# Moving the next batch's projections and its q transfer ahead inside an attention and FFN kernel

## The chip, the cores and the metric

One core of a Trainium2 chip runs the kernel. The metric is the device time of one execution in microseconds.

## The reference

Four batches of 512 tokens with 128 channels pass through one transformer block: layer norm, attention with 16 heads of 8 channels, a residual, layer norm, a mixture FFN whose eight experts are all computed, and a residual.

```python
qkv = (x @ w_attn + b_attn).reshape(b, t, 3, H, D).transpose(2, 0, 3, 1, 4)
scores = jnp.einsum('bhtd,bhsd->bhts', q, k) / jnp.sqrt(jnp.float32(D))
scores = scores + slopes[None, :, None, None] * pos[None, None, None, :]
attn = jax.nn.softmax(jnp.where(causal[None, None], scores, -jnp.inf), axis=-1)
y = jnp.einsum('bhts,bhsd->bhtd', attn, v)            # then @ w_proj + b_proj
x = x + attention(layernorm(x))
logits = xf @ gate_w.T + gate_b                       # xf = layernorm(x), rows of 128
logits = logits * rsqrt(mean(logits * logits) + eps) * rms_w
g = top_1(softmax(logits / 0.5)); norm_g = g / (g + 1e-6)
h = gelu(einsum('nd,edh->neh', xf, w1) + b1); y = einsum('neh,ehd->ned', h, w2) + b2
x = x + (y * norm_g[:, None, None]).sum(axis=1)
```

## The kernel before

The work is laid out by hand. A batch has four steps (s = 0 to 3), one for each set of four heads, and each step has 16 places. Tables say at which place each engine takes which piece: the two plans give the twelve units of maxima, the twelve units of scores and exponentials and the three kinds of attention times v; `STAGES` (L72) gives the stages that come once per batch as (step, place, batches behind; -1 is the next batch). Every engine walks the same tables in its own program, so an engine's order is fixed and all coupling is through semaphores.

In a step, TensorE computes raw scores of the next step's heads for the row maxima (`max_unit`, L720, into three banks `v_ring` which VectorE empties at L1047), transposes the maxima (L729), and computes this step's scores again (`exp_unit`, L742 and L748, into three banks `a_ring`) for ScalarE's exponentials (L553), then multiplies them with v (L767). The negated maxima take part in the scores as rows of `q_stack`: VectorE writes `m_hi` and `m_lo` (L1064, L1065), SP sends them with `load_max` (L385), and the first scores of the next step, at its place 4, wait for them. FFN tiles of an earlier batch (L673 to L675 into `a_ring`, gelu at L570, L835) are spread over the steps from batch 1 step 1 on: five in a step, but one in each step 2.

The next batch's x is prepared on the way. VectorE takes its statistics (`x_stats`, L958), GpSimd the inverse root (`x_rstd`, fourteen small operations at L330 to L341), VectorE normalises (`x_norm`, L967), TensorE transposes (`x`, L684) and projects (`k` and `q` at L673 to L675, `v` the same lines in twelve small products), VectorE evacuates (L950, L951, L1019, L1011, L1033). q and k are split into a high part (ScalarE, L594, at the units of `SCALAR_STAGES`) and a low part (GpSimd, `split_low`, L442). They go to the operands `q_stack` (two buffers) and `k_stack` (one) by DMA: `load_q` (L366, 256 KB each: the high part twice and the low part once; from batch 2 on also 64 KB of zeros, L362, ahead), `load_k` on SP for the high key parts (L324, eight of 32 KB for each half of the heads) and `load_k_low` on GpSimd (L324, four of 32 KB). The first half of `k_stack` is free for the next batch when all scores of steps 0 and 1 are out. The first maxima of the next batch stand at place 0 of step 3 and wait for q and both key parts.

SP's program inside the loop is `load_k(b, 1)`, `load_residual(b)`, `load_x(b + 1)` in step 0; `store(b - 2)` in step 1, which waits for the result of the stage `ffn` at place 14 of that step; the loads of the next batch in step 2; and `load_max` at the end of each step. GpSimd's has `load_k_low(b, 1)` and the inverse root of z in step 0 and, in step 1, `x_rstd`, both `split_low` and `norm_logits(b - 1)` (L330 to L341, L482, L483), which waits for the logits of place 4 of step 2; then `load_k_low(b + 1, 0)` and `residual(b)` in step 2.

Of the kernel before, what the change touches and what calls it, by code (L numbers as in the profile page):

```python
# [71 lines left out]
STAGES = {  # L72
    "y_low": (2, 14, 0), "y_high": (0, 4, 1), "y_norm": (0, 5, 1), "attention": (0, 7, 1),
    "z_norm": (0, 13, 1), "z": (0, 15, 1), "logits": (2, 4, 1), "route": (2, 13, 1), "gates": (3, 13, 1),
    "ffn": (1, 14, 2), "x_stats": (0, 15, -1), "x_norm": (1, 7, -1), "x": (1, 10, -1), "k": (1, 12, -1),
    "q": (1, 15, -1), "v": (1, 14, -1), "b2": (2, 15, 0),
}

SCALAR_STAGES = {
    "k_high": (1, 7, -1), "q_high": (1, 11, -1), "gates": (3, 1, 1),  # L80
}


# [14 lines left out]
def block_kernel(nc, x, w_attn, w_proj, w1, w2, columns, rows, consts, out):  # L98
    B, T, C = x.shape
# [19 lines left out]
    with ExitStack() as ctx:  # L119
# [169 lines left out]
        def next_set(b, s):  # L289

            return (b, s + 1) if s < SETS - 1 else (b + 1, 0)
# [29 lines left out]
        def send_k(queue, part, half, g, q, loaded):  # L321

            rows = QR * q + half * QR // 2
            queue.dma_start(k_stack[QR * g + q * D:QR * g + (q + 1) * D, 2 * half:2 * half + 2, q, :].bitcast(F32),  # L324
                            part[rows:rows + QR // 2, :].bitcast(F32)).then_inc(loaded, 16)

        def inverse_sqrt(engine, settle, y, src, scale, eps, v, t, fused=False):


            settle(engine.tensor_scalar(v, src, scale, eps, ALU.mult, ALU.add))  # L330
            settle(engine.tensor_scalar(y.bitcast(I32), v.bitcast(I32), -0.5, float(RSQRT_GUESS), ALU.mult, ALU.add))
            for _ in range(3):
                if fused:
                    settle(engine.scalar_tensor_tensor(out=t, in0=y, scalar=-0.5, in1=y, op0=ALU.mult, op1=ALU.mult))
                    settle(engine.tensor_tensor(t, t, v, ALU.mult))
                    settle(engine.scalar_tensor_tensor(out=y, in0=t, scalar=1.5, in1=y, op0=ALU.add, op1=ALU.mult))
                else:
                    settle(engine.tensor_tensor(t, y, y, ALU.mult))
                    settle(engine.tensor_tensor(t, t, v, ALU.mult))
                    settle(engine.tensor_scalar(t, t, -0.5, 1.5, ALU.mult, ALU.add))  # L340
                    settle(engine.tensor_tensor(y, y, t, ALU.mult))  # L341
# [4 lines left out]
        @block.sync  # L346
        def _(sp):
            def load_x(b):
                if b >= 1:
                    sp.wait_ge(xn_ready, b)  # L350
                sp.dma_start(x_in[:], x_view[b]).then_inc(x_loaded, 16)

            def load_residual(b):
                if b >= 1:
                    sp.wait_ge(xb_ready, b)
                sp.dma_start(x_res[:], x_view[b]).then_inc(xres_loaded, 16)

            def load_q(b):

                if b >= 2:  # L360
                    sp.wait_ge(e_filled, UNITS * SETS * (b - 1))
                    sp.dma_start(q_stack[b % 2][MAX_ROWS:MAX_ROWS + 2 * QUADS, :, :].bitcast(F32),  # L362
                                 zeros[0:2 * QUADS * SETS, :]).then_inc(q_loaded, 16)
                for g, part in ((0, 0), (1, 0), (2, 1)):
                    sp.wait_ge(q_split, 2 * b + part + 1)
                    sp.dma_start(q_stack[b % 2][QR * g:QR * (g + 1), :, :].bitcast(F32),  # L366
                                 (q_hi, q_lo)[part][:].bitcast(F32)).then_inc(q_loaded, 16)

            def load_k(b, half):


                if b == 0:
                    sp.wait_ge(k_zeros, half + 1)
                else:

                    sp.wait_ge(e_filled, UNITS * (SETS * (b - 1) + 2 * half + 2))
                sp.wait_ge(k_split, 2 * b + 1)
                for q in range(QUADS):
                    for g in (0, 2):
                        send_k(sp, k_hi, half, g, q, k_loaded[half][q])  # L380

            def load_max(b, s):
                sp.wait_ge(m_ready, SETS * b + s + 1)
                for r, part in ((MAX_ROWS, m_hi), (MAX_ROWS + QUADS, m_lo)):
                    sp.dma_start(q_stack[b % 2][r:r + QUADS, s, :].bitcast(F32),  # L385
                                 part[:].bitcast(F32)).then_inc(m_loaded, 16)

            def store(b):
                sp.wait_ge(result_ready, b + 1)
                sp.dma_start(out_view[b], result[:]).then_inc(stored, 16)  # L390

            load_x(0)
            sp.dma_start(w_attn_sb[:], w_attn).then_inc(wa_loaded, 16)
            sp.dma_start(cst[:], consts).then_inc(cst_loaded, 16)
            sp.dma_start(cols_sb[:], columns).then_inc(rows_loaded, 16)
            sp.dma_start(rows_sb[:], rows.to_broadcast([P, rows.shape[1]])).then_inc(rows_loaded, 16)
            sp.dma_start(w1_sb[:], w1).then_inc(w1_loaded, 16)
            load_q(0)
            load_k(0, 0)
            load_k(0, 1)  # L400
            sp.dma_start(w_proj_sb[:], w_proj).then_inc(wp_loaded, 16)
            sp.dma_start(w2_sb[:], w2).then_inc(w2_loaded, 16)
            load_residual(0)
            load_x(1)
            load_max(0, 0)
            for b in range(B):
                for s in range(SETS):
                    if s == 0 and b >= 1:
                        load_k(b, 1)
                        load_residual(b)  # L410
                        if b + 1 < B:
                            load_x(b + 1)
                    if s == 1 and b >= 2:
                        store(b - 2)
                    if s == 2 and b + 1 < B:
                        load_k(b + 1, 0)
                        load_q(b + 1)
                    if next_set(b, s)[0] < B:
                        load_max(*next_set(b, s))
            store(B - 2)  # L420
            store(B - 1)
            sp.wait_ge(stored, 16 * B)
# [3 lines left out]
        def _(pool):  # L426
# [22 lines left out]
            def load_k_low(b, half):  # L449

                if b == 0:
                    pool.wait_ge(k_zeros, half + 1)
                else:

                    pool.wait_ge(e_filled, UNITS * (SETS * (b - 1) + 2 * half + 2))
                pool.wait_ge(k_split, 2 * b + 2)
                for q in range(QUADS):
                    send_k(pool, k_lo, half, 1, q, k_low_loaded[half][q])
# [3 lines left out]
            def settle(ins):  # L462

                steps[0] += 1
                ins.then_inc(pool_step, 1)
                pool.wait_ge(pool_step, steps[0])
# [11 lines left out]
            def norm_logits(b):  # L478

                pool.wait_ge(square_ready, b + 1)  # L480
                inverse_sqrt(pool, settle, inverse_rms[:], mean_square[:], 1.0 / E, EPS_F32, var[:, 0, :], var[:, 1, :])
                settle(pool.tensor_tensor(lg2[:], lg[:], inverse_rms[:].unsqueeze(2).to_broadcast([P, TB, E]), ALU.mult))  # L482
                pool.tensor_tensor(lg[:], lg2[:], rms_rows.unsqueeze(1).to_broadcast([P, TB, E]),  # L483
                                   ALU.mult).then_inc(logits_normed, 1)
# [29 lines left out]
            for b in range(B):  # L514
                for s in range(SETS):
                    if s == 0 and b >= 1:
                        load_k_low(b, 1)
                        z_rstd(b - 1)
                    if s == 1 and b + 1 < B:
                        x_rstd(b + 1)  # L520
                        split_low(b + 1, 0)
                        split_low(b + 1, 1)
                    if s == 1 and b >= 1:
                        norm_logits(b - 1)
                    if s == 2 and b + 1 < B:
                        load_k_low(b + 1, 0)
                    if b == 0 and s == 0:
                        pool.wait_ge(w1_loaded, 16)
                        split(w1_sb[:], w1_hi[:], w1_lo[:], w1_split, 0)
                        pool.wait_ge(rows_loaded, 32)  # L530
                        split(gate_sb, gate_parts[:, 0:E], gate_parts[:, E:2 * E], w1_split, 2)
                    if s == 2:
                        residual(b)
# [744 lines left out]
```

## Time and profile before

| what | value |
|---|---|
| median of 3 runs | 341.61 us (341.31 to 342.7) |
| profiled execution, span | 341.4 us |
| TensorE busy | 295.9 us (87%) |
| VectorE busy | 192.6 us (56%) |
| ScalarE busy | 193.7 us (57%) |
| GpSimd busy | 84.1 us (25%) |
| mean granted clock of TensorE | 0.949 |
| idle of TensorE ahead of L720, until the low key parts landed | 15.3 us in 3 stretches, the longest 8.9 |

The span runs from the first to the last instruction of one execution. Busy shares are of the whole span. An idle time is put down to what came last. The longest of the three stretches is in the start of the kernel. The engines are named PE (TensorE), PEld (its weight loads), DVE (VectorE), ACT (ScalarE), POOL (GpSimd) and SP (SyncE); a q behind the name is the engine's sequencer.

### The profile page before, as it was taken

How to read it: one execution, taken by the hardware profiler on the slowest of the kernel's cores; microseconds unless marked ns; L12 is line 12 of the kernel's file. 1: busy time of each engine (PE TensorE's matmuls, PEld its weight loads, DVE VectorE, ACT ScalarE, POOL GpSimd, SP SyncE). 2: the span in 40 equal slices, each digit the busy share in tenths (PEclk: the TensorE clock that was granted, in tenths of full speed). 3: DMA queues.
4: the chain of work that ended last, by engine and by line, in shares of the span. 5: the costliest groups of instructions: out<-in, count | busy, mean ns of one | idle time of the engine just before them, and what ended most of it. 6: DMA issues, size and time to landing. Idle time of an engine off the chain costs nothing.

```text
span 341.4 us, 5507 instructions
## 1 busy us (share of the span) xinstructions
PE 295.9 (87%) x1784; PEld 193.8 (57%) x1784; DVE 192.6 (56%) x787; ACT 193.7 (57%) x322; POOL 84.1 (25%) x213
## 2 busy tenths in 40 slices
PE   0245899997979999699999997899999999998994
PEld 0133466565556676466766765557756665655661
DVE  5624759776786867145677776264867741161111
ACT  1871064463455568275759467376667788634462
POOL 8569203240233027002033126002210220000030
PEclk9985579999999999699999999899999999999999
DMA  7166500070120006200300028001100100000101
GB/s 198 66 90 96 193 2 2 16 122 9 38 74 4 0 19 105 29 2 18 95 1 4 0 61 120 3 2 44 35 4 2 35 2 2 0 2 0 31 1 31
DMA packets 12380, 13.29 MB, mean 39 GB/s; under 512 B 2048, under 2 KB 9088, under 8 KB 12096
## 3 DMA queue, kind: packets, MB, share of 16 engines
q1 hardware_dynamic: 11328, 11.90, 16.1%
q0 software_dynamic: 1024, 1.05, 1.9%
q8 instruction: 14, 0.23, 0.3%
q14 instruction: 14, 0.11, 0.1%
HBM read 5.21 MB, written 1.05 MB: 18 GB/s over the span
## 4 chain that ended last, share of the span: by engine, by line
PE 74%; DVE 12%; DMA 7%; issue 3%; ACT 1%; POOL 1%; DVEq 0%; SPq 0%; ACTq 0%; POOLq 0%
PE ffn_bank L835 16%; PE a_ring L742 11%; PE v_ring L720 11%; PE pv_bank L767 9%; DMA k_stack<-k_lo 6%; PE a_ring L673 5%; DVE unused L1047 5%; PE a_ring L748 5%; PE a_ring L674 4%; PE a_ring L675 4%; DVE xn L967 2%; PE v_ring L796 1%; PE v_ring L729 1%; DMA x_in<-x 1%; PE v_ring L673 1%
## 5 line engine op out<-in xcount | busy, mean ns | idle before, releaser
L1047 DVE CUSTOM_DVE_ANT_0 unused<-v_ring,cst 128x512 bf16<-128x512 f32 (+3 forms) x256 | 112.1, 487 | 68.5 <-PE v_ring L720 63.9
L553 ACT ACTIVATE probs<-a_ring 128x512 f32<-128x512 f32 (+1 forms) x192 | 92.5, 526 | 74.7 <-PE a_ring L748 73.5
L720 PE MATMUL v_ring<-k_stack,q_stack 128*128 128x512 f32 (+3 forms) x256 | 89.6, 422 | 20.2 <-DMA k_stack<-k_lo 15.3
L742 PE MATMUL a_ring<-q_stack,k_stack 128*128 128x512 f32 (+3 forms) x256 | 76.8, 360 | 0.4 <-DMA q_stack<-m_lo 0.4
L720 PEld LDWEIGHTS v_ring<-k_stack,q_stack 128*128 128x128 f32 x256 | 49.5, 210 | 40.6 <-issue 23.5
L570 ACT ACTIVATE hidden<-a_ring,cols_sb 128x512 f32<-128x512 f32 x64 | 43.4, 688 | 43.2 <-PE a_ring L675 42.7
L835 PE MATMUL ffn_bank<-hidden,w_sb 128*128 128x512 f32 x128 | 66.3, 602 | 1.1 <-ACT ffn_T L579 0.8
L742 PEld LDWEIGHTS a_ring<-q_stack,k_stack 128*128 128x128 f32 x256 | 46.7, 197 | 7.8 <-issue 4.0
L748 PE MATMUL a_ring<-score_mask,ident_bf 128*128 128x128 bf16 (+1 forms) x192 | 48.1, 252 | 0.0
L767 PE MATMUL pv_bank<-probs,v_ones 128*32 128x256 f32 (+3 forms) x512 | 43.2, 447 | 0.0
L673 PE MATMUL a_ring<-zT_hi,w_hi 128*128 128x512 f32 x64 | 34.2, 534 | 0.8 <-DVEq L953 0.8
L324 POOL DMA_DIRECT2D k_stack<-k_lo x32 | 18.1, 568 | 61.3 <-PE a_ring L748 60.5
L748 PEld LDWEIGHTS a_ring<-score_mask,ident_bf 128*128 128x128 bf16 x192 | 18.7, 98 | 20.6 <-issue 14.0
L674 PE MATMUL a_ring<-zT_lo,w_hi 128*128 128x512 f32 x64 | 26.1, 407 | 0.0
L675 PE MATMUL a_ring<-zT_hi,w_lo 128*128 128x512 f32 x64 | 25.9, 405 | 0.0
L835 PEld LDWEIGHTS ffn_bank<-hidden,w_sb 128*128 128x128 f32 x128 | 21.5, 192 | 5.9 <-ACT hidden L570 3.1
L1047 DVE DVE_READ_ACCUMULATOR2_ANT row_max<- 128x1 f32 x256 | 21.3, 83 | 0.0
L673 PEld LDWEIGHTS a_ring<-zT_hi,w_hi 128*128 128x128 f32 x64 | 12.7, 199 | 12.3 <-issue 7.9
L330 POOL TENSOR_SCALAR var<-mean_square 128x4 f32<-128x4 f32 x4 | 0.8, 193 | 73.8 <-DVE mean_square L1113 73.8
L767 PEld LDWEIGHTS pv_bank<-probs,v_ones 128*32 128x32 f32 x512 | 12.4, 110 | 10.0 <-issue 7.0
L570 ACT ACT_TABLE_LOAD x13 | 16.7, 1283 | 0.2
L674 PEld LDWEIGHTS a_ring<-zT_lo,w_hi 128*128 128x128 f32 x64 | 12.8, 200 | 5.0 <-issue 3.6
(109 smaller groups left out, 298.4 us busy)
## 6 DMA issues: line engine op xcount, KB each, us to landing
q_stack<-q_hi SPq DMA_DIRECT2D x8, 256.0 KB
k_stack<-k_hi SPq DMA_DIRECT2D x64, 32.0 KB
x_in<-x SPq DMA_DIRECT2D x4, 256.0 KB, 3.6
hidden<-w SPq DMA_DIRECT2D x1, 1024.0 KB, 8.3
q_stack<-q_lo SPq DMA_DIRECT2D x4, 256.0 KB
k_stack<-k_lo POOLq DMA_DIRECT2D x32, 32.0 KB, 4.0
w_sb<-w SPq DMA_DIRECT2D x1, 1024.0 KB, 5.2
x_res<-x SPq DMA_DIRECT2D x4, 256.0 KB, 3.1
```

The lines of the kernel that those rows point to most:

```text
L324: queue.dma_start(k_stack[QR * g + q * D:QR * g + (q + 1) * D, 2 * half:2 * half + 2, q, :].bitcast(F32), part[rows:rows + QR // 2, :].bit ...
L553: act.activation(probs[:, n % 2, q, KIND_AT[kind]:KIND_AT[kind] + cols], a_bank()[:, 0:cols], ACT.Exp).then_inc(e_freed, 1)
L570: act.activation(hidden[:, n % HB, :], a_bank()[:], ACT.Gelu, bias=b1_cols[:, m:m + 1]).then_inc(g_freed, 1)
L673: pe.matmul(dst, lhs[0], rhs[0], start=True, stop=False)
L674: pe.matmul(dst, lhs[0], rhs[1], start=False, stop=False)
L675: return pe.matmul(dst, lhs[1], rhs[0], start=False, stop=True)
L720: last = pe.matmul(dst[:, at:at + P * (n + 1)], q_stack[b % 2][:, s, n * P:(n + 1) * P], k_stack[:, s, q, 0:P * (n + 1)], start=True, stop ...
L742: pe.matmul(dst[:, at:at + P * (TB - j)], k_stack[:, s, q, j * P:(j + 1) * P], q_stack[b % 2][:, s, j * P:T], start=(at == 0), stop=False, ...
L748: pe.matmul(diagonal, ident_bf[:], score_mask[:].unsqueeze(1).to_broadcast([P, blocks, P]), start=False, stop=True, skip_group_check=True) ...
L767: last = pe.matmul(pv_bank[QR * q:QR * (q + 1), j * P:T], v_ones[b % 2][:, j, s, q, :], probs[:, n % 2, q, at:at + cols], start=(s % 2 == ...
L835: pe.matmul(ffn_bank[:], w2_sb[:, m, :], hidden[:, n % HB, :], start=(m == 0), stop=(m == NT - 1)).then_inc(ffn2_done, 1)
L1047: ins = dve.tensor_tensor_reduce(unused[:, (uses[0] - 1) % V_BANKS, at:at + cols], bank_[:, at:at + cols], cst[:, C_MASK + T - cols:C_MASK ...
```

## The change

The next batch's stages move: the statistics from place 15 of step 0 to place 9, the normalisation from place 7 of step 1 to place 0, the transpose from 10 to 3, k from 12 to 5, q from 15 to 7, v from 14 to 10; the high parts on ScalarE move from behind unit 7 (k) and 11 (q) of step 1 to behind units 2 and 4. SP sends q in step 1, behind the store and ahead of the maxima, where it sent it in step 2 behind the high key parts. GpSimd sends the low key parts ahead of the normalisation of the logits.

```diff
-    "ffn": (1, 14, 2), "x_stats": (0, 15, -1), "x_norm": (1, 7, -1), "x": (1, 10, -1), "k": (1, 12, -1),
-    "q": (1, 15, -1), "v": (1, 14, -1), "b2": (2, 15, 0),
+    "ffn": (1, 14, 2), "x_stats": (0, 9, -1), "x_norm": (1, 0, -1), "x": (1, 3, -1), "k": (1, 5, -1),
+    "q": (1, 7, -1), "v": (1, 10, -1), "b2": (2, 15, 0),
 }
 
 SCALAR_STAGES = {
-    "k_high": (1, 7, -1), "q_high": (1, 11, -1), "gates": (3, 1, 1),
+    "k_high": (1, 2, -1), "q_high": (1, 4, -1), "gates": (3, 1, 1),
 }
...
                     if s == 1 and b >= 2:
                         store(b - 2)
+                    if s == 1 and b + 1 < B:
+                        load_q(b + 1)
                     if s == 2 and b + 1 < B:
                         load_k(b + 1, 0)
-                        load_q(b + 1)
                     if next_set(b, s)[0] < B:
                         load_max(*next_set(b, s))
...
-                    if s == 1 and b >= 1:
-                        norm_logits(b - 1)
                     if s == 2 and b + 1 < B:
                         load_k_low(b + 1, 0)
+                    if s == 2 and b >= 1:
+                        norm_logits(b - 1)
```

## Rows read from the trace of the kernel before

**Rows 1.** The page: its first line, and the granted clock in 40 slices.

```profile
span 341.4 us, 5507 instructions
...
PEclk9985579999999999699999999899999999999999
```

**Rows 2.** Timeline, TensorE: start us, us, what, idle before and releaser.

```profile
79.00 0.70 PE L720 MATMUL v_ring<-k_stack,q_stack 128*128 128x512 f32 x3 [2.77 <-issue]
...
139.70 1.19 PE L720 MATMUL v_ring<-k_stack,q_stack 128*128 128x512 f32 x3 [3.12 <-DMA k_stack<-k_lo]
...
214.57 1.19 PE L720 MATMUL v_ring<-k_stack,q_stack 128*128 128x512 f32 x3 [3.22 <-DMA k_stack<-k_lo]
```

**Rows 3.** Timeline, GpSimd: the issue of batch 2's low key parts.

```profile
133.49 2.27 POOL L324 DMA_DIRECT2D k_stack<-k_lo  x4 [0.32 <-PE a_ring L748]
```

**Rows 4.** Windows: busy us of PE, PEld, DVE, ACT, POOL; granted clock; DMA; GB/s.

```profile
139.00:140.00 1.00, 0.30 (x1) 0.33 (x2) 0.00 (x0) 0.00 (x0) 0.00 (x0) 0.64 0.02 4
...
146.00:147.00 1.00, 1.00 (x6) 0.85 (x5) 0.02 (x1) 0.82 (x2) 0.00 (x0) 0.95 0.00 0
...
217.00:218.00 1.00, 1.00 (x4) 0.76 (x4) 0.00 (x0) 0.00 (x0) 0.00 (x0) 0.61 0.00 0
```

**Rows 5.** Timeline, the SP queue: issues.

```profile
72.17 0.61 SPq L366 DMA_DIRECT2D q_stack<-q_lo  x1
...
196.63 0.39 SPq L390 DMA_DIRECT2D out<-result  x1
...
204.67 0.67 SPq L362 DMA_DIRECT2D q_stack<-zeros  x1
...
206.67 0.60 SPq L366 DMA_DIRECT2D q_stack<-q_lo  x1
```

**Rows 6.** Timeline, TensorE and VectorE, batch 2, steps 1 and 2.

```profile
194.79 0.30 PE L673 MATMUL v_ring<-w_attn_hi,xT_hi 128*128 128x128 f32 x1
...
195.33 1.13 DVE L1136 SCALAR_TENSOR_TENSOR result<-v_ring,gate,x 128x128 f32<-128x128 f32 x4 [0.26 <-DVE m_lo L1065]
...
196.16 1.07 PE L835 MATMUL ffn_bank<-hidden,w_sb 128*128 128x512 f32 x2
...
197.24 0.48 PE L673 MATMUL v_ring<-xT_hi,w_attn_hi 128*128 128x512 f32 x1
...
198.03 0.63 PE L720 MATMUL v_ring<-k_stack,q_stack 128*128 128x512 f32 x3
...
203.40 0.44 PE L742 MATMUL a_ring<-q_stack,k_stack 128*128 128x512 f32 x1
```

**Rows 7.** Chain near 39 us; DMA issues with us to landing, 30:45, then 90:100.

```profile
39.26 1.91 DMA q_stack<-m_lo
...
x_in<-x SPq DMA_DIRECT2D x1, 256.0 KB, 5.6
...
x_in<-x SPq DMA_DIRECT2D x1, 256.0 KB, 3.1
```

**Rows 8.** Timeline, VectorE, batch 1, end of step 0.

```profile
98.57 0.69 DVE L1047 CUSTOM_DVE_ANT_0 unused<-v_ring,cst 128x512 bf16<-128x512 f32 x1
...
101.80 1.12 DVE L967 TENSOR_SCALAR z<-x,mv,rstd 128x128 f32<-128x128 f32 x4 [0.33 <-POOLq L476]
...
105.40 0.87 DVE L958 BATCH_NORM_STATS2 stats<-x_in 128x6 f32<-128x128 f32 x4 [0.32 <-DVE zT_lo L951]
...
106.61 0.66 DVE L1047 CUSTOM_DVE_ANT_0 unused<-v_ring,cst 128x512 bf16<-128x512 f32 x1
```

**Rows 9.** Timeline, batch 0, end of step 1 and step 2.

```profile
63.29 0.28 DVE L1065 SCALAR_TENSOR_TENSOR m_lo<-v_ring,m_hi 16x128 fp32r<-16x128 f32 x1
...
65.09 0.75 DVE L1011 TENSOR_SCALAR q_full<-v_ring,cols_sb 128x512 f32<-128x512 f32 x1 [0.32 <-PE v_ring L675]
...
67.11 1.28 POOL L442 TENSOR_TENSOR q_lo<-q_full,q_hi 128x512 fp32r<-128x512 f32 x1 [2.26 <-ACT q_hi L594]
...
68.29 0.44 PE L742 MATMUL a_ring<-q_stack,k_stack 128*128 128x512 f32 x1
```

## The prediction

> **What bounds the kernel now.** I read the page first, then the idle time of TensorE in the timeline around each start of a batch's work, then the SP and GpSimd queues there, then the clock by windows. The span is 341.4 us and the granted clock is low only at the start and in two short dips [rows 1]; TensorE is busy 87% of the span, so what matters is where it stands still. It does so at one place of each batch: step 3, place 0, where the first maxima of the next batch need that batch's q and k in SBUF. The idle times in brackets are 2.77, 3.12 and 3.22 us for next batches 1, 2 and 3, so it stopped at 76.23, 136.58 and 211.35 [rows 2]. The releaser named is the low key parts: GpSimd issues them only at 133.49, as it first normalised the logits of the batch before [rows 3]. But SP sends q late too: from the issue of its low part to TensorE's restart it is 6.83 us at batch 1 (72.17 to 79.00) and 7.90 us at batch 3 (206.67 to 214.57) [rows 2, 5]. Both have to come earlier, and the change moves both.
>
> In the two later stalls the clock fell to 1.2 GHz (0.5 of full). Window 139 to 140 has a mean of 0.64, which puts the fall at 139.3, 2.7 us after the stop; the windows at 146 and 217 put the return at 146.1 and 217.8 [rows 4]. From restart to return that is 6.4 and 3.2 us at half speed, in which TensorE is the bound: 3.2 and 1.6 us lost.
>
> **What the change gives.** q, k and v leave places 12 to 15 of step 1 for 5, 7 and 10, q is issued in step 1, and the low key parts no longer wait for the logits. The key parts then go out when the last scores of step 1 are done, some 12 us ahead of the stop. SP's eight issues of high key parts follow the maxima's, as before. None of these is last at step 3 any more. Stalls: 2.77 + 3.12 + 3.22 = 9.1 us. Clock: 3.2 + 1.6 = 4.8 us. Span 341.4 - 13.9 = 327.5 us if nothing takes their place. Behind the stalls the next limit is TensorE itself: ScalarE and VectorE were idle in them. The number of instructions is the same on every engine. GpSimd's normalisation of the logits now follows four key issues, and its reader stands at place 13 of step 2, so it costs nothing.
>
> **What it costs, part by part.** I take the edits in order of time.
>
> *Batch 0, step 1.* This step has no FFN tiles and VectorE nearly fills it. v and q ran behind the maxima (the negated maxima end at 63.57; v at 63.89, q at 65.09, 0.88 and 0.75 us with gaps of 0.3 us) and now run ahead of them, 2.2 us; the statistics of 1.2 us leave the step and add some 0.5 us to the one before. So the negated maxima are ready at about 65.1. q's part on VectorE ends five maxima units and v ahead of them, some 5 us, at 60.2; from its end to the end of GpSimd's low part was 2.55 us (65.84 to 68.39), so SP issues that part at about 62.8 and it is usable 6.83 us later, at 69.6. The maxima, issued at 65.3, lie behind it in SP's queue. The first scores of step 2 need them and started at 68.29 [rows 5, 9]. Cost 1.3 us; bounds 0 (the end of VectorE's excess is covered) and 2.5.
>
> *Batch 1, step 0.* The statistics of the next x move from place 15 to place 9. On VectorE they take from 105.40 to the next operation at 106.61, 1.2 us. Place 9 comes there at 98.57. What follows is tight: the maxima, then z at 101.80 after only 0.33 us of idle, and TensorE waited for z [rows 8]. So z comes some 1.3 us later, and with it TensorE's next FFN tiles. Bounds 0.9 (the 0.33 us absorb a part) and 2.1 (x not yet landed when its statistics come; x takes 3.1 us there [rows 7]).
>
> *Batch 2, step 0, and the order inside the steps 1 with FFN tiles.* There VectorE has gaps and TensorE is the bound. ScalarE takes the high key parts after unit 2 and may wait a little for VectorE, with three banks of scores as a cover. I put 0.4 us, bounds -0.5 and 1.5.
>
> *Batch 2, step 1: the store.* This is the large one. In SP's program the store of batch 0's result stands ahead of the new q loads, and it waits for the FFN result of place 14. Before, only the maxima of step 2 stood behind it. Now the store, the zeros, q's three transfers and then the maxima leave in this order, though q itself has long been ready. The result op ran at 195.33 and the store went at 196.63. v and q now stand ahead of it on TensorE, which has no idle time there: v takes 194.79 to 196.16, 1.37 us, and q 197.24 to 198.03, 0.79 us [rows 5, 6]. So the store goes at 198.8, the zeros at 199.2, and the low q part 2.0 us later (204.67 to 206.67 before [rows 5]), at 201.2. By the two distances of the first paragraph q is usable at 208.1 to 209.1. The maxima were issued behind it. If they land behind it, the first scores of step 2, which started at 203.40 [rows 6], wait until 208.7: 5.3 us, bounds 4.7 and 5.8. If they pass it, they go at 201.9 and 202.6 and land 1.91 us later [rows 7], at 204.5: 1.1 us. For the first speaks that a 256 KB load of x takes 5.6 us on this queue behind a 1 MB load and 3.1 us without [rows 7]; I take 5.3. TensorE has nothing else to do in that time, and 5.3 us is longer than the 2.7 us after which the clock fell before, so I add the mean of the two losses, 2.4 us (bounds 1.6 and 3.2). Sum 7.7 us; this batch alone loses what its old stall cost (3.2 + 1.6) and more.
>
> The Trainium skill (DMA: Bandwidth & Descriptors, section Queues, rings and completion order) says that on each DMA engine descriptors are consumed in ring order, and that SP has one ring on each of the engines. By that rule the maxima's packets wait behind q's, and this case's x rows agree (5.6 against 3.1 us); it speaks against putting q ahead of the maxima. By the rule the sum would be the forecast, without it the time of the first rival.
>
> At batch 1 there is no store ahead. There q's part on VectorE also ends five maxima units and v ahead of the maxima, as in batch 0, and the step holds five FFN tiles more, so I put nothing.
>
> **Sum.** 327.5 + 1.3 + 1.3 + 0.4 + 7.7 = 338.2 us of span. The median of the runs, 341.61, is 0.2 above the profiled span, so 338.4 us.
>
> **Rivals.**
> *The maxima pass q* (or the store comes early enough): in batch 2 the cost is 1.1 us without a clock fall: 338.4 - 4.2 - 2.4 = 331.8 us. For it: the maxima are 8 KB and no row shows them behind q with a reader waiting. Against: the x rows. Chance 0.2. It reaches down to 328 if the costs of batches 0 and 1 are nil as well.
> *The clock falls in batch 1 too.* With z 1.3 us later, two idle stretches follow each other around 98 to 104. The clock held through 2.77 us of idle at batch 1's stall, as the page's clock line shows no dip there [rows 1, 2], but these two are close together. Price 1.6 to 3.2: 340.8 us. Chance 0.12.
> *SP is held at q in every batch* (slower). If the low q part is ready not 5 us ahead of the maxima, but 2 us behind them, because ScalarE's high part or GpSimd's low part is late, then SP stands at that wait with the maxima ready behind it. At batch 0 the low part goes at 67.1 and the scores at 73.9: 5.6 instead of 1.3 us. At batch 1, by the distances of batch 2's rows (maxima ready at 195.1 + 2.2, q part at 199.2, usable at 207.1, scores at 203.40), 3.7 us and a clock fall of 2.4. Sum 338.4 + 4.3 + 6.1 = 348.8 us. It decides as soon as the q part is later than the maxima by about 0.5 us. Against it: on VectorE q is five units and v ahead of the maxima. Chance 0.06.
> *The stalls stay,* because something else is last at step 3 (the high key parts, eight issues of SP that follow the maxima). They would have to be some 4 us later than I put them. In batch 2, where SP is late with them, TensorE is late as well. One of the two larger stalls kept, with its clock, gives 338.4 + 3.1 + 3.2 = 344.7 us. Chance 0.04.
>
> **How the numbers follow.** Forecast 338.4 us, chance 0.58, own range 336 to 340.5. The range for 8 in 10 reaches to the first and second rival: 330.5 to 341.5. A measurement of this kernel can tell about 0.5% from no change, so faster is below 339.9 and slower above 343.3. Faster: nearly all of the forecast, the first rival and a third of the second, 0.83. Slower: 0.07. Within: 0.10.
>
> **What would show it.** Right: no idle time of TensorE at step 3, place 0, in any batch; key issues of GpSimd right behind the last scores of step 1; in batch 2 the store some 2 us later than its place now, and then an idle stretch of about 5 us ahead of the first scores of step 2 with the maxima's transfer as releaser, and a clock dip behind it; in batch 1 z 1.3 us later in its step. Wrong: if that stretch is 1 us, packets pass each other in SP's queue; if TensorE still waits at step 3, a key part is last; if the steps 1 of batches 0 and 1 show waits of the scores for maxima longer than 2 us, the third rival holds.

## The result and the profile after

The changed kernel takes 342.52 us (median of 20 runs, 339.45 to 345.44) and the kernel before 341.69 us (20 runs); the ratio, from which executions over 1.5% above the fastest of their kernel are left out, is 1.005 with a 95% interval of 1.0028 to 1.0073, and that of the two medians is 1.002. So it is slower, by half a per cent or less. The forecast was 338.4 us, faster by 1%, with a range up to 341.5. Two parts of the page of the changed kernel, for [rows 1]: the totals, TensorE's busy share in 40 slices and the granted clock in tenths of full speed.

```profile
span 341.0 us, 5507 instructions
...
PE 298.7 (88%) x1784; PEld 195.8 (57%) x1784; DVE 190.3 (56%) x787; ACT 194.9 (57%) x322; POOL 84.7 (25%) x213
...
PE   0607999799959999999999929999999999998994
...
PEclk9965599989998999999999976999999999999999
```

The span is even 0.4 us shorter than in the profile of before, 341.0 against 341.4 us. That is an accident of the start, which the change does not touch: the first scores of batch 0 came at 41.30 us in the profile of before and at 37.9 to 38.6 us in that of every other kernel of this text. So the two profiles have to be compared step by step. The table has the start of the first scores of each step (the first product of `exp_unit`, at place 4), read from the timeline, and the interval since the one ahead. Below, an interval is named by the batch and step at whose first scores it ends: (2, 2) is the 18.59 us up to the first scores of batch 2, step 2.

| batch, step | before, us | interval | after, us | interval | difference |
|---|---|---|---|---|---|
| 0, 0 | 41.30 | | 38.03 | | |
| 0, 1 | 53.78 | 12.48 | 51.09 | 13.06 | +0.6 |
| 0, 2 | 68.29 | 14.51 | 67.45 | 16.36 | +1.9 |
| 0, 3 | 81.29 | 13.00 | 79.26 | 11.81 | -1.2 |
| 1, 0 | 91.57 | 10.28 | 89.54 | 10.28 | 0.0 |
| 1, 1 | 110.45 | 18.88 | 111.53 | 21.99 | +3.1 |
| 1, 2 | 128.63 | 18.18 | 129.44 | 17.91 | -0.3 |
| 1, 3 | 148.80 | 20.17 | 143.56 | 14.12 | -6.1 |
| 2, 0 | 166.12 | 17.32 | 160.88 | 17.32 | 0.0 |
| 2, 1 | 184.81 | 18.69 | 180.01 | 19.13 | +0.4 |
| 2, 2 | 203.40 | 18.59 | 204.60 | 24.59 | +6.0 |
| 2, 3 | 222.19 | 18.79 | 221.79 | 17.19 | -1.6 |
| 3, 0 | 239.51 | 17.32 | 239.11 | 17.32 | 0.0 |

Behind (3, 0) the two agree to 0.1 us a step. The differences add up to +2.9 us. The medians differ by 0.8 us only: the profile of before was a quick execution but for its start, and the part on the sum says what is known of that.

The stalls at step 3 are gone, as meant. The two sums of TensorE's idle time by releaser (us in total, times, longest) show what came for them: of the key parts only the wait in the kernel's start is left, and the scores now wait for the maxima.

```profile
PE v_ring L721 <- DMA k_stack<-k_lo: 8.9, 1, 8.9
...
PE a_ring L743 <- DMA q_stack<-m_lo: 8.5, 3, 6.1
```

This is step 3, place 0 of batch 1, which answers to the second line of [rows 2]: the products of the maxima follow the products with v without idle time.

```profile
136.32 1.07 PE L768 MATMUL pv_bank<-probs,v_ones 128*32 128x384 f32 x16
...
137.32 0.74 PE L721 MATMUL v_ring<-k_stack,q_stack 128*128 128x512 f32 x3
```

And these are the places where TensorE waits instead (timeline; the idle time ahead of each in brackets): the first scores of (0, 2); the transposes of the maxima and of z at the end of batch 1's step 0; the last maxima ahead of, and the first scores of, (2, 2).

```profile
67.45 0.49 PE L743 MATMUL a_ring<-q_stack,k_stack 128*128 128x512 f32 x1 [1.94 <-DMA q_stack<-m_lo]
...
99.70 0.28 PE L730 MATMUL v_ring<-cst,row_max 128*16 128x128 f32 x1 [1.09 <-DVEq L1057]
...
102.10 1.12 PE L805 MATMUL v_ring<-cst,z 128*128 128x128 f32 x4 [1.45 <-DVE z L968]
...
197.68 0.80 PE L721 MATMUL v_ring<-k_stack,q_stack 128*128 128x384 f32 x2
...
204.60 0.80 PE L743 MATMUL a_ring<-q_stack,k_stack 128*128 128x512 f32 x1 [6.12 <-DMA q_stack<-m_lo]
```

In batch 1 only the 1.09 us ahead of the maxima's transpose are new. The wait for z is as long in the profile of before, where it had no fall of the clock:

```profile
102.97 0.66 PE L804 MATMUL v_ring<-cst,z 128*128 128x128 f32 x4 [1.45 <-DVE z L967]
```

The wait ahead of (2, 2) is the store's. VectorE's result op and SP's queue behind it, for [rows 5, 6]:

```profile
192.26 1.13 DVE L1137 SCALAR_TENSOR_TENSOR result<-v_ring,gate,x 128x128 f32<-128x128 f32 x4 [0.27 <-PE v_ring L843]
```

```profile
193.57 0.39 SPq L390 DMA_DIRECT2D out<-result  x1
194.01 0.70 SPq L362 DMA_DIRECT2D q_stack<-zeros  x1
194.75 1.24 SPq L366 DMA_DIRECT2D q_stack<-q_hi  x2
196.04 0.60 SPq L366 DMA_DIRECT2D q_stack<-q_lo  x1
196.69 0.68 SPq L385 DMA_DIRECT2D q_stack<-m_hi  x1
197.41 0.85 SPq L385 DMA_DIRECT2D q_stack<-m_lo  x1
```

The store goes 0.2 us behind the result, then the zeros, q and the maxima, in one row. The maxima, issued at 196.69 and 197.41, are usable at 204.60. In the chain that ended last their second part takes 7.15 us there and 3.77 us in batch 0:

```profile
63.64 3.77 DMA q_stack<-m_lo
...
197.41 7.15 DMA q_stack<-m_lo
```

And the clock falls at each of the three places: in batch 0 0.4 us after TensorE's restart, in the other two while TensorE still waits. The windows, for [rows 4], have the granted clock third from the end:

```profile
core 0: us, PE busy (x) PEld busy (x) DVE busy (x) ACT busy (x) POOL busy (x), PEclk, DMA share, GB/s
...
67.00:68.00 1.00, 0.55 (x3) 0.40 (x3) 0.00 (x0) 0.00 (x0) 0.00 (x0) 0.91 0.17 37
...
71.00:72.00 1.00, 1.00 (x10) 0.92 (x8) 0.71 (x5) 0.49 (x2) 0.00 (x0) 0.89 0.14 33
...
101.00:102.00 1.00, 0.00 (x0) 0.00 (x0) 1.00 (x4) 0.98 (x2) 0.68 (x4) 0.97 0.00 0
...
102.00:103.00 1.00, 0.90 (x5) 0.90 (x5) 0.05 (x1) 0.44 (x1) 0.75 (x4) 0.50 0.06 16
...
105.00:106.00 1.00, 1.00 (x20) 0.38 (x12) 1.00 (x3) 0.00 (x0) 0.00 (x0) 0.82 0.00 0
...
200.00:201.00 1.00, 0.00 (x0) 0.00 (x0) 0.00 (x0) 0.00 (x0) 0.69 (x4) 0.97 1.07 127
...
201.00:202.00 1.00, 0.00 (x0) 0.00 (x0) 0.00 (x0) 0.00 (x0) 0.70 (x4) 0.50 1.05 129
...
211.00:212.00 1.00, 1.00 (x10) 0.92 (x8) 0.76 (x4) 0.71 (x2) 0.00 (x0) 0.91 0.00 0
```

It is at 0.5 from about 67.8 to 71.2, from 101.9 to 105.4, and from 200.9 to 211.2 us.

### The profile page after: what moved, and what is told of

Same layout as the page of the kernel before. It is cut to its first block, busy times and chain, and to the rows that moved or that the text cites. A ratio compares the mean times of both kernels' runs of the same rounds, so it can differ in the third digit from the quotient of the medians.

```text
span 341.0 us, 5507 instructions
## 1 busy us (share of the span) xinstructions
PE 298.7 (88%) x1784; PEld 195.8 (57%) x1784; DVE 190.3 (56%) x787; ACT 194.9 (57%) x322; POOL 84.7 (25%) x213
## 3 DMA queue, kind: packets, MB, share of 16 engines
q1 hardware_dynamic: 11328, 11.90, 16.3%
## 4 chain that ended last, share of the span: by engine, by line
PE 71%; DMA 8%; DVE 8%; SPq 4%; ACT 4%; issue 3%; POOL 2%; DVEq 0%; ACTq 0%; POOLq 0%
PE ffn_bank L836 15%; PE a_ring L743 11%; PE v_ring L721 10%; PE pv_bank L768 9%; PE a_ring L674 5%; PE a_ring L749 4%; PE a_ring L676 4%; PE a_ring L675 4%; DMA q_stack<-m_lo 4%; DVE unused L1048 4%; DMA k_stack<-k_lo 2%; DMA cst<-consts 2%; SPq L324 2%; ACT k_stack L604 1%; PE v_ring L674 1%
## 5 line engine op out<-in xcount | busy, mean ns | idle before, releaser
L554 ACT ACTIVATE probs<-a_ring 128x512 f32<-128x512 f32 (+1 forms) x192 | 93.9, 526 | 90.6 <-PE a_ring L749 89.4
L721 PE MATMUL v_ring<-k_stack,q_stack 128*128 128x512 f32 (+3 forms) x256 | 91.9, 430 | 11.1 <-DMA k_stack<-k_lo 8.9
L743 PE MATMUL a_ring<-q_stack,k_stack 128*128 128x512 f32 (+3 forms) x256 | 78.9, 369 | 8.5 <-DMA q_stack<-m_lo 8.5
L721 PEld LDWEIGHTS v_ring<-k_stack,q_stack 128*128 128x128 f32 x256 | 50.9, 216 | 31.3 <-issue 21.6
L743 PEld LDWEIGHTS a_ring<-q_stack,k_stack 128*128 128x128 f32 x256 | 48.2, 203 | 16.8 <-DMA q_stack<-m_lo 8.5
L749 PE MATMUL a_ring<-score_mask,ident_bf 128*128 128x128 bf16 (+1 forms) x192 | 49.2, 257 | 0.0
L674 PE MATMUL a_ring<-zT_hi,w_hi 128*128 128x512 f32 x64 | 33.0, 516 | 0.8 <-DVEq L954 0.8
L675 PE MATMUL a_ring<-zT_lo,w_hi 128*128 128x512 f32 x64 | 25.1, 393 | 0.0
L675 PEld LDWEIGHTS a_ring<-zT_lo,w_hi 128*128 128x128 f32 x64 | 12.1, 189 | 4.9 <-issue 3.6
```

The lines of the kernel that those rows point to most:

```text
L554: act.activation(probs[:, n % 2, q, KIND_AT[kind]:KIND_AT[kind] + cols], a_bank()[:, 0:cols], ACT.Exp).then_inc(e_freed, 1)
L674: pe.matmul(dst, lhs[0], rhs[0], start=True, stop=False)
L675: pe.matmul(dst, lhs[0], rhs[1], start=False, stop=False)
L721: last = pe.matmul(dst[:, at:at + P * (n + 1)], q_stack[b % 2][:, s, n * P:(n + 1) * P], k_stack[:, s, q, 0:P * (n + 1)], start=True, stop ...
L743: pe.matmul(dst[:, at:at + P * (TB - j)], k_stack[:, s, q, j * P:(j + 1) * P], q_stack[b % 2][:, s, j * P:T], start=(at == 0), stop=False, ...
L749: pe.matmul(diagonal, ident_bf[:], score_mask[:].unsqueeze(1).to_broadcast([P, blocks, P]), start=False, stop=True, skip_group_check=True) ...
```

## The experiments

Each run is told by the intervals of the table above where its profile decides, and by its time beside runs of the kernel before on the same chip.

**1. q ahead of the store.** The changed kernel with two calls exchanged in SP's step 1:

```diff
+                    if s == 1 and b + 1 < B:
+                        load_q(b + 1)
                     if s == 1 and b >= 2:
                         store(b - 2)
-                    if s == 1 and b + 1 < B:
-                        load_q(b + 1)
```

> The changed kernel with one edit: in step 1, SP sends the next batch's q ahead of the store instead of behind it. Theory A (in batch 2 the store holds q, so that the maxima end up behind 832 KB of q traffic): the 6.12 us of idle ahead of the first scores of batch 2's step 2 and the clock dip behind it go; that step's interval falls from 24.6 to about 18.6 us and the next from 17.2 to about 14; time about 342.5 - 9 = 333.5 us. The waits of batch 0 (1.94 us) and of batch 1 stay. Rival B (the maxima are late by themselves, because v and q stand ahead of them on TensorE): the store's place changes nothing, 4 us or more of idle stay and the time is above 338 us.

Measured: 333.12 us against 340.51 of before, ratio 0.976 (0.971 to 0.981). The intervals of (2, 2) and (2, 3) fall from 24.59 and 17.19 to 18.31 and 14.11 us, 9.4 us together, and no idle time is left there. The wait of batch 0 stays, as expected, and the clock dip behind it was longer in this profile ((0, 3) is 13.17 us):

```profile
68.29 0.80 PE L743 MATMUL a_ring<-q_stack,k_stack 128*128 128x512 f32 x1 [2.20 <-DMA q_stack<-m_lo]
```

So the place of the store alone turns the changed kernel from 0.5% slower into 2.4% faster.

**2. q behind the maxima.** The changed kernel with q still in step 1, but behind the maxima:

```diff
-                    if s == 1 and b + 1 < B:
-                        load_q(b + 1)
...
                     if next_set(b, s)[0] < B:
                         load_max(*next_set(b, s))
+                    if s == 1 and b + 1 < B:
+                        load_q(b + 1)
```

> The changed kernel with SP sending the next batch's q in step 1 behind the maxima of that step instead of ahead. Theory A (the maxima wait behind q in SP's queue in batches 0 and 2): both idle times ahead of the first scores of step 2 go (1.94 and 6.12 us) with their clock dips; q still lands before step 3 in batches 1 and 2, and within 1 us of it in batch 0; about 331.5 us. Rival: q and with it the high key parts, now behind it, land too late for step 3, and stalls of 1 to 3 us come back there in each batch with clock dips: 336 to 340 us.

Measured: 329.62 us, ratio 0.966 (0.961 to 0.971). (0, 2) is 14.56 us instead of 16.36, (0, 3) 10.25 instead of 11.81; batch 2 is as in the first run; no stall at step 3. The maxima of batch 0 did wait behind q. What is left is mostly in batch 1, where (1, 1) is 22.24 us against 18.88 before. The page's clock line shows a dip there and nowhere else:

```profile
PEclk9999999999997999999999999999999999999999
```

**3. GpSimd's order alone.** The kernel before, with the low key parts ahead of the normalisation of the logits, everything else as it was:

```diff
-                    if s == 1 and b >= 1:
-                        norm_logits(b - 1)
                     if s == 2 and b + 1 < B:
                         load_k_low(b + 1, 0)
+                    if s == 2 and b >= 1:
+                        norm_logits(b - 1)
```

> The kernel before with the GpSimd part of the change alone: low key parts sent ahead of the normalisation of the logits; stages and SP's order as before. Theory A (two transfers are late at step 3, and q's low part is as late as the low key parts): the stalls stay at 2.8 to 3.2 us, perhaps 1 us shorter as key and q traffic no longer meet; 340 to 341.7 us. Rival (the low key parts alone were last, as the page names them): the stalls of batches 1 and 2 and their clock dips go, 8 us less, about 333.5 us.

Measured: 338.39 us against 340.51, ratio 0.991 (0.988 to 0.995). The three stalls are all there, 0.4 to 0.5 us shorter in batches 1 and 2, and those two are now put down to q's low part:

```profile
75.63 0.70 PE L720 MATMUL v_ring<-k_stack,q_stack 128*128 128x512 f32 x3 [2.77 <-issue]
...
137.56 0.73 PE L720 MATMUL v_ring<-k_stack,q_stack 128*128 128x512 f32 x3 [2.73 <-DMA q_stack<-q_lo]
...
210.60 0.97 PE L720 MATMUL v_ring<-k_stack,q_stack 128*128 128x512 f32 x3 [2.68 <-DMA q_stack<-q_lo]
```

So the releaser that the page named in [rows 2] was only the last of two: the other transfer, q's low part, was 0.4 to 0.5 us earlier. Behind the first stall the clock fell, which it had not done in the profile of before: the page's clock line shows it, and (1, 0) is 11.77 us instead of 10.28.

```profile
PEclk9965599997999999799999999799999999999999
```

**4. Late statistics.** The run with q behind the maxima, and all moved stages some places later:

```diff
-"x_stats": (0, 9, -1), "x_norm": (1, 0, -1), "x": (1, 3, -1), "k": (1, 5, -1), "q": (1, 7, -1), "v": (1, 10, -1)
+"x_stats": (0, 15, -1), "x_norm": (1, 3, -1), "x": (1, 6, -1), "k": (1, 8, -1), "q": (1, 10, -1), "v": (1, 12, -1)
-"k_high": (1, 2, -1), "q_high": (1, 4, -1)
+"k_high": (1, 5, -1), "q_high": (1, 7, -1)
```

> The run with q behind the maxima, and the next batch's stages three places later: statistics back at place 15 of step 0, normalisation 3, transpose 6, k 8, q 10, v 12 of step 1, high parts behind units 5 and 7. Theory A (the statistics at place 9 delay z in batch 1 and with it bring the clock dip there): batch 1's interval from the first scores of step 0 to those of step 1 falls from 22.0 to about 19.2 us, the clock dip near 102 us goes, 2.8 us less than with the stages of the change. Rival (the clock dip there is chance, or comes from the rest of the change): no more than 1.2 us less.

Measured: 337.97 us (eight runs, one of them 422.1 us), ratio 0.989 (0.985 to 0.994), 8 us slower than the run it started from. In batch 1 it did as expected: (1, 1) is 18.87 us, 3.4 less. But (0, 2) is 22.79 us instead of 14.56, and (1, 2) and (2, 2) are 1.9 and 1.7 us longer. In batch 0 the statistics' root isn't ready at place 3, VectorE stands with the maxima behind it, TensorE with it; the clock is at half for about 10 us there (0.50 in all windows from 54 to 62 us). The maxima are late again ahead of the scores:

```profile
54.76 1.09 PE L685 MATMUL v_ring<-cst,xn 128*128 128x128 f32 x4 [2.91 <-DVE row_max L1048]
...
73.27 0.50 PE L743 MATMUL a_ring<-q_stack,k_stack 128*128 128x512 f32 x1 [1.73 <-DMA q_stack<-m_lo]
```

The expectation for batch 1 held and that for the whole did not: I had not looked at what the later normalisation meets in batch 0.

**5. Statistics late in one batch only.** The run with q behind the maxima; `due` looks up two stages of batch 2's x at other places:

```diff
+    moved = {("x_stats", 2): (0, 13), ("x_norm", 2): (1, 2)}
     return [(name, b - behind) for name, (step, place, behind) in stages.items()
-            if (s, k) == (step, place) and 0 <= b - behind < batches]
+            if (s, k) == moved.get((name, b - behind), (step, place)) and 0 <= b - behind < batches]
```

> The run with q behind the maxima, with the statistics of batch 2's x alone at place 13 of step 0 (right behind z's normalisation) instead of place 9, and their normalisation at place 2 of step 1 instead of 0. Theory A (the statistics at place 9 of batch 1 delay z, and the clock dip follows from that): batch 1's interval up to the first scores of step 1 falls from 22.2 to 19.5 us and the dip near 100 us goes; 327.0 us. Rival (VectorE then waits for the root at place 2 and gives the gain back, as in the run with late statistics): 329 to 331 us.

Measured: 328.37 us, ratio 0.966 (0.961 to 0.971); beside the 329.62 of experiment 2, which ran beside other runs of before, that is no difference to rely on. (1, 1) is 20.28 us and the clock line shows no dip. It lies between theory (19.5) and the 22.24 us of experiment 2: z is on time, but VectorE waits 1.1 us for the root and TensorE 0.56 us for the normalised x.

**6. Fewer bytes ahead of the maxima.** The changed kernel, with the second of q's three transfers for batch 3 cut to one row of 2 KB:

```diff
+                    if b == B - 1 and g == 1:
+                        sp.dma_start(q_stack[b % 2][QR * g:QR * g + 1, 0:1, :].bitcast(F32),
+                                     q_hi[0:1, :].bitcast(F32)).then_inc(q_loaded, 16)
+                        continue
```

> The changed kernel, with the second of the three q transfers for batch 3 cut from 256 KB to 2 KB, its place in SP's queue kept (so batch 3's scores lack the product of the high q part with the low key part). Theory A (the maxima of batch 2's step 2 land behind the bytes of q ahead of them): at 131 bytes per ns 254 KB less are 2.0 us less, so the idle time ahead of the first scores falls from 6.1 to 4.1 us. Rival B (they wait for SP's issues or for a fixed latency, not for q's bytes): it stays at 5.5 to 6.1 us.

Measured in one profile (its run took 338.36 us), the first scores of (2, 2):

```profile
200.91 0.80 PE L747 MATMUL a_ring<-q_stack,k_stack 128*128 128x512 f32 x1 [4.16 <-DMA q_stack<-m_lo]
```

4.16 us instead of 6.12, 1.96 less for 254 KB less, where 2.0 were expected. The issues had the same number and length, so the maxima wait for the bytes of q ahead of them. The second profile of the changed kernel (experiment 9) has 6.32 us in this place, so the figure is good to some 0.2 us.

**7. GpSimd's old order.** The run with q behind the maxima, with `norm_logits` ahead of `load_k_low` as in the kernel before:

> The run with q behind the maxima, with GpSimd's order as before the change (logits normalised ahead of the low key parts). Theory A (GpSimd's order is a limit of its own at step 3 once q is early): the low key parts are issued some 4.8 us behind the first scores of step 2 and usable about 5 us later, so idle times of 1 to 3 us come back at step 3 of batches 1 and 2, partly with clock dips; 333 to 336 us. Rival (q alone was what counted): no idle there, 329.6 us.

Measured: 331.72 us, ratio 0.979 (0.971 to 0.986), 2.1 us more than with the new order. The stall comes back in batch 2, where the issue and TensorE's restart are these, and (2, 3) is 16.05 instead of 14.12 us; in batch 1 it does not ((1, 3) is 14.19):

```profile
198.66 2.39 POOL L324 DMA_DIRECT2D k_stack<-k_lo  x4 [0.32 <-PE a_ring L749]
...
203.63 0.70 PE L721 MATMUL v_ring<-k_stack,q_stack 128*128 128x512 f32 x3 [1.88 <-DMA k_stack<-k_lo]
```

Restart comes 5.0 us behind the issue. The limit exists, but it is smaller and in fewer batches than expected, and the time is below the 333 to 336 us of the theory. The same run tells something on the clock: its wait for z in batch 1 is as long as in experiment 2 (1.26, 1.18 and 1.44 us in three pieces against 1.26, 1.19 and 1.50), yet no slice of its clock line is below 9 and (1, 1) is 20.61 us, 1.6 less than 22.24.

**8. Only the order of the transfers.** The kernel before with the edit of experiment 3 and one more, no stage moved:

```diff
                     if s == 2 and b + 1 < B:
-                        load_k(b + 1, 0)
                         load_q(b + 1)
+                        load_k(b + 1, 0)
```

> The kernel before with no stage moved: GpSimd's low key parts ahead of the normalisation of the logits, and on SP q ahead of the high key parts in step 2. Theory A (what is late at step 3 is only the order of the transfers, so the moved projections are not needed and their costs in batches 0 and 1 are saved): q's low part is issued some 6 us earlier and all parts land ahead of step 3 in batches 1 and 2; in batch 0 an idle time of about 1.3 us stays; the interval of batch 1's step 1 stays at 18.9 us; 327 to 329 us. Rival (the high key parts, now behind 768 KB of q, become the last): idle times of 2 us or more stay at step 3 with clock dips, 334 to 338 us.

Measured: 327.30 us (four runs, 326.99 to 327.61) against 340.38 of before, ratio 0.962 (0.957 to 0.967): 3.8% faster than the kernel before and 4.4% less than the changed kernel's median, which was taken beside other runs of before. In batch 0 an idle time of 0.97 us is left at step 3; (1, 3) and (2, 3) are 14.12 us as with q a step ahead; (1, 1) is 18.89 us as before.

```profile
73.51 0.71 PE L720 MATMUL v_ring<-k_stack,q_stack 128*128 128x512 f32 x3 [0.97 <-issue]
```

This is SP's queue in batch 1, step 2, where q's low part leaves 4.9 us behind the second part of the maxima (116.08) and 10 us ahead of TensorE's first maxima of step 3 (131.03):

```profile
119.61 1.24 SPq L366 DMA_DIRECT2D q_stack<-q_hi  x2
120.97 0.55 SPq L366 DMA_DIRECT2D q_stack<-q_lo  x1
121.64 6.44 SPq L324 DMA_DIRECT2D k_stack<-k_hi  x8
129.84 0.64 SPq L385 DMA_DIRECT2D q_stack<-m_hi  x1
```

**9. The changed kernel again,** without an edit.

> The changed kernel once more, unedited, for a second profile. Theory A (the idle times are the kernel's, the length of each clock dip behind them is chance): ahead of the first scores the same idle times as before (1.9 to 2.2 us in batch 0, 6.1 in batch 2), while the intervals that hold a dip (batch 0 steps 2 and 3, batch 1 step 1, batch 2 step 3) differ by up to 1.6 us from the first profile. Rival: the idle times differ by over 1 us, so that one profile can't be read to that.

Measured in one run of 341.53 us: idle times of 2.16 and 6.32 us (1.94 and 6.12 in the first profile). (0, 3) is 10.25 instead of 11.81 us; the others that hold a dip, (1, 1) and (2, 3), are within 0.15 us. So the waits are the kernel's, and the dip behind the wait of (0, 2) comes and goes, for 1.6 us.

**10. q's projection ahead of v's,** on top of experiment 8:

```diff
-    "q": (1, 15, -1), "v": (1, 14, -1), "b2": (2, 15, 0),
+    "q": (1, 14, -1), "v": (1, 15, -1), "b2": (2, 15, 0),
-    "k_high": (1, 7, -1), "q_high": (1, 11, -1), "gates": (3, 1, 1),
+    "k_high": (1, 7, -1), "q_high": (1, 10, -1), "gates": (3, 1, 1),
```

> The kernel before with both orders of transfers changed and no projection moved (the run before this group), and q's projection ahead of v's: q at place 14, v at 15 of step 1, q's high part behind unit 10. Theory A (in batch 0 what is left at step 3 is the landing of the key parts behind q, 0.97 us): q is ready about 1.2 us earlier, the idle time goes, 326.3 us. Rival (v is then late for its first product, or ScalarE waits for q behind unit 10 and holds up exponentials): 327 us or more.

Measured: 327.24 us (six runs), ratio 0.958 (0.954 to 0.963) to its own runs of before, the same time as experiment 8. The 0.97 us at step 3 are gone, (0, 2) is 0.7 us longer: ScalarE waits for q, and the scores for a free bank.

```profile
59.76 0.38 PE L742 MATMUL a_ring<-q_stack,k_stack 128*128 128x256 f32 x1 [0.59 <-ACT probs L553]
```

**11. Early statistics alone,** in the kernel before:

```diff
-"x_stats": (0, 15, -1)
+"x_stats": (0, 9, -1)
```

> The kernel before with one edit: the statistics of the next x at place 9 of step 0 instead of 15. Theory A (they stand ahead of z's chain in batch 1): the interval up to batch 1's first scores of step 1 grows from 18.9 to about 20.2 us, and to 22 us if the clock dips there; batch 2's by no more than 0.2 us. Rival (the cost of 3.1 us in that interval came from the moved transpose and projections): 18.9 to 19.2 us.

Measured in one profile (its run took 343.77 us): (1, 1) is 21.66 us with a clock dip in it, (2, 1) 18.69 as before. So 2.8 of the 3.1 us that batch 1 lost are the statistics' and not the projections'. The profile has a second finding that was not looked for, in batch 0. The stall at its step 3 is 2.72 us, as in [rows 2], but this time the clock fell behind it, as in experiment 3: (1, 0) is 13.01 us instead of 10.28.

```profile
75.02 0.71 PE L720 MATMUL v_ring<-k_stack,q_stack 128*128 128x512 f32 x3 [2.72 <-issue]
...
100.78 0.28 PE L729 MATMUL v_ring<-cst,row_max 128*16 128x128 f32 x1 [1.13 <-DVEq L1056]
```

## Why the prediction was wrong

**What the change gives: right.** The forecast was 13.9 us. Taking the intervals without stall or dip from experiments 2 and 8, the old stalls and dips were worth 2.75 us at (0, 3), 6.05 at (1, 3) and 4.67 at (2, 3), 13.5 us together. That both transfers had to move was right too: experiment 3 moved one and the stalls stayed, experiment 7 put one back and 2.1 us came back, far less than the old stalls were worth.

**That the gain needs the moved projections: not claimed, but not asked either.** I costed the change as a whole. Experiment 8 has the same gain from the two orders of transfers with every projection at its old place, and is 2.3 us below experiment 2 and 1.1 us below experiment 5, the best version with moved ones.

**The store: the mechanism was right, the term mis-sized.** Forecast 5.3 us of idle and 2.4 of clock; measured against experiment 1, 6.3 in the interval of (2, 2) (24.59 against 18.31) and 3.1 behind it in that of (2, 3) (17.19 against 14.11), 9.4 against 7.7 us. The idle time ended 8.6 us behind the issue of q's low part (196.04 to 204.60). I had taken the distances of [rows 5], 6.8 and 7.9 us, which end at a reader of q, and put nothing on the maxima's own way behind it. The rival that the maxima pass q is refuted by experiment 6, and experiment 1 shows the store as the cause: 9.4 us. The rule of the Trainium skill (DMA: Bandwidth & Descriptors, section Queues, rings and completion order) that the descriptors of a ring are consumed in order agrees with this, 1.96 us for 254 KB.

**Batch 0: mis-sized.** Forecast 1.3 us. Measured 0.6 in (0, 1), 1.8 in (0, 2) and 1.6 in (0, 3) against experiment 2's 10.25: 4.0 us. That q goes ahead of the maxima and is ready when I put it was right. With the 3.3 us of the early start added, SP issued q's low part at 62.3 (forecast 62.8) and the maxima at 66.2 (65.3), so it was not held:

```profile
59.03 0.55 SPq L366 DMA_DIRECT2D q_stack<-q_lo  x1
...
62.93 0.66 SPq L385 DMA_DIRECT2D q_stack<-m_hi  x1
```

What was off is again the landing: the scores started 8.4 us behind the issue of q's low part (59.03 to 67.45), where I had taken 6.83. They waited for the second part of the maxima, 3.77 us behind its issue; how much of that is q's bytes in this batch no run tells. The idle time was 1.94 us, and the clock fell behind it, which I had excluded there: I had read from one profile that 2.77 us of idle leave the clock alone. Experiments 3 and 11 show the same wait with a fall and [rows 2] without one. That reading is the step that failed; the length of one idle time doesn't settle it.

**Batch 1: the chain right, the clock wrong.** Forecast 1.3 us for z, and a second rival with a clock fall (chance 0.12). Measured +3.1 in (1, 1). Of seven profiles with the early statistics (both of the changed kernel, experiments 1, 2, 6, 7 and 11) two have no dip there and 20.56 and 20.61 us, 1.7 more than before. Five have the dip and 21.66 to 22.24 us. Of the 1.7 us, 0.3 come back in (1, 2), where the transpose of x no longer stands; so the delay itself is 1.4 us, near the 1.3 of the forecast. The rival with the clock fall had to be the likelier case.

**The sum.** So the terms of the costs were mis-sized, the clock's above all: 16.3 us instead of 10.7. Batch 0 4.0 for 1.3; batch 1 3.1 - 0.3 = 2.8 and (2, 1) with its part in (2, 2) 0.44 - 0.28 = 0.2, together 3.0 for 1.7; the store 9.4 for 7.7. Of the 5.6 us of difference 3.7 are clock dips (1.6 in batch 0, 21.99 - 20.6 = 1.4 in batch 1, 3.1 - 2.4 = 0.7 in batch 2) and most of the rest the landing behind q. 16.3 less the 13.5 gained is, to rounding, the 2.9 us of the table. Set against the 13.9 us forecast, that is 6 us for two profiled executions, while the median missed the forecast by 4.1. The 2 us between lie in the executions of before: in every run with both numbers the time is 1.8 us above the span, so the median of before answers to a span of 339.9 us, and its profile, without a start that was some 3.3 us late, to one of 338.1. Experiments 3 and 11 kept the stall of batch 0 and lost 1.5 and 2.7 us to the clock behind it, which that profile did not; where the other executions of before lose their time is not on record. The third rival, SP held at q in every batch, did not happen in batches 0 and 1. What was missing is not a mechanism but a case: all the waits that I had named, each with a clock dip behind it.

## What to carry to other kernels

A transfer moved ahead in a queue takes everything behind it along: list for each batch what stands ahead of it in the new place and waits (here a store), and what stands behind it and is small and urgent (here two transfers of 8 KB of maxima behind 832 KB). When a stall names one transfer, look for the second one that lands just ahead of it, and try the order of the queues before moving the computation that feeds them. Cost a new wait on TensorE with its clock dip.

## What the runs showed of the hardware

The same wait can bring the clock down or not: 2.72 to 2.77 us of idle in batch 0 cost nothing behind it in the profile of before, 1.5 us in experiment 3 and 2.7 us in experiment 11; 1.9 to 2.2 us of idle in (0, 2) cost 1.6 us in one profile of the changed kernel, nothing in the other and in experiment 6, and 2.9 us in experiment 1. In batch 1 three waits of 1.0 to 1.5 us close together brought the clock down in five of seven profiles; with the first and the last of them alone, as in before and in experiments 3, 4, 8 and 10, it did not fall. From a wait of 6.12 us the clock returned 6.6 us after TensorE's restart. I had expected a fall only behind the long waits.

The start differs too. In the first profile of the changed kernel the granted clock was 0.50 from about 20 to 44 us, in its second profile 1.00 throughout that stretch, yet both reach the first scores of batch 0 at 38.0 us. Nineteen of the 20 executions of the changed kernel fall into two groups by mean granted clock, seven at 0.978 to 0.982 with a median of 341.3 us and twelve at 0.938 to 0.947 with 342.7; the second profile belongs to the first group and the first to the second. Between these two profiles the dip behind (0, 2) makes the difference in time.
